# Summing a unit's four neighbour slots by accumulating gathers, with a ring of 16 units, in a three-layer MoE graph network and two attention layers

## The chip, the cores and the metric

One core of a Trainium2 chip. The metric is the device time of one execution in microseconds (us); the median of the timed runs counts. Nothing outside the kernel's one launch is measured.

## The reference, cut to what matters

A graph of N = 6250 nodes and E = 106250 edges sorted by target. Three layers of a mixture of experts each take the mean of the neighbours' hidden rows (256 float32), choose two of eight experts, and add the result to the row. Two attention layers (GAT) follow, the first with four heads.

```python
for l in range(L):                                   # L = 3, h is [N, 256]
    agg = jax.ops.segment_sum(h[src], dst, num_segments=N) / deg
    logits = jnp.concatenate([h, agg], axis=-1) @ router_W[l] + router_b[l]
    vals, idx = jax.lax.top_k(logits, TOPK)
    ...
    h = h + conf * moe
return h @ W_out + b_out
```

```python
e = jax.nn.leaky_relu(alpha_s[src] + alpha_d[dst], NEG_SLOPE)
ex = jnp.exp(e - m[dst])
out = jax.ops.segment_sum(h[src] * alpha[:, :, None], dst, num_segments=n)
```

In the MoE layers only the sum of the neighbours' rows is needed. In the GAT layers each row is weighed with its own softmax weight, so the rows have to arrive one by one.

## The kernel before, in words

**Tiling.** The nodes are sorted by degree and dealt out to 49 groups of 128 nodes (one node to a partition). A group's edges are padded to its own greatest degree and cut into units of four slots (`SLOTS = 4`, line 46). One slot is one indirect DMA: 128 rows, one to a partition, taken from a table in HBM by 128 indices out of `stage`. The trace has 657 real units in the three MoE rounds, 219 to a round (4.47 to a group), filled up to 224 units, which are 896 gathers to a round. There are five such rounds: three of MoE with rows of 256 floats, two of GAT with rows of 136 floats.

**The ring.** `ring` (line 98) holds 32 slots, eight units. GpSimd's queue (POOL) issues the gathers in the loop of lines 466 to 480: unit by unit, slot by slot, each signed off on the unit's own semaphore `gathered[u]`. In the middle of each unit POOL waits twice: at line 473 on `ring_free` (DVE has used up the old contents of the next unit) and at line 475 on `gathered` of the unit before, after which it raises `arrived` for DVE. SyncE (SP) reloads half of `stage` (16 slots) once the units of that half have arrived (lines 358 to 362).

**MoE rounds on DVE.** `aggregate` (lines 686 to 702) starts from the node's own row (line 692), and per unit waits on `arrived`, sums the four slots of the unit with a TENSOR_REDUCE (line 696, which frees the unit), and adds the partial sum to the accumulator in PSUM (line 699). Beside this DVE gates the experts of the group before the last (line 710), adds up the weak experts (line 713), forms the gates of the last group (lines 729 to 749, in which line 738 waits for ACT's exponential), and adds the strong experts to h (line 723). PE transposes the operands of group g (lines 1216 to 1220), runs the first products of group g-1 (line 1243), the router, the weak experts and the second products of group g-2 (line 1284). `fill_up` (line 677) passes over the units of padding at a round's end.

**Between rounds** POOL waits until each group's h is done and scatters it to the next table (line 492: 49 indirect DMAs, line 496 for the GAT tables); the next round's gathers begin when all have landed.

**GAT rounds on DVE.** Per unit a score, a running maximum, the weights (exponential on ACT), the weighing (line 866, which frees the unit) and the sum (line 870). At a group's end comes `turn` (line 872).

```python
                        if b % SLOTS == SLOTS // 2:
                            pool.wait_ge(ring_free, i * UNITS + (b // SLOTS + 2))
                            pool.wait_ge(gathered[(b // SLOTS - 1) % UNITS], i * (16 * SLOTS) + 16 * SLOTS)
                            pool.sem_inc(arrived, 1)
```

Of the kernel before, what the change touches and what calls it, by code (L numbers as in the profile page):

```python
# [26 lines left out]
ALU = mybir.AluOpType  # L27
# [19 lines left out]
RING = 32  # L47
# [20 lines left out]
def gnn_kernel(nc, x, src, dst, W_in, b_in, router_W, router_b, weak_W, weak_b, strong_W1, strong_b1,  # L68
# [3 lines left out]
    with ctx:  # L72
# [25 lines left out]
        ring = sb("ring", [P, RING, H])  # L98
# [4 lines left out]


# [28 lines left out]
        hist = sb("hist", [GROUPS, 3, P])  # L133
# [8 lines left out]
        zeros = sb("zeros", [P, P])  # L142
# [73 lines left out]
        def bank(name):  # L216
# [24 lines left out]
        half_begun, arrived, round_gathered, ring_free, table_done = (sem(n) for n in (  # L241
            "half_begun", "arrived", "round_gathered", "ring_free", "table_done"))
# [30 lines left out]
        def _(sp):  # L273
# [60 lines left out]
            for r in range(LAYERS + 2):  # L334
# [22 lines left out]
                with sp.Fori(1, bodies) as i:  # L357
                    for half in range(2):
                        sp.wait_ge(arrived, total * r + i * UNITS + (r + 1 - UNITS + (half + 1) * UNITS // 2))
                        sp.dma_start(stage[:, half, :], slot_tab[:, bass.ds(i * RING + half * RING // 2, RING // 2)])\  # L360
                            .then_inc(staged[half], 16)
# [4 lines left out]
        def _(pool):  # L366
# [48 lines left out]
            for g in range(GROUPS):  # L415
                pool.indirect_dma_start(out=run_raw[:, g, :], out_offset=None, in_=src.rearrange("(a e) -> a e", a=1),
                                        in_offset=bass.IndirectOffsetOnAxis(ap=perm[:, g, 1:2], axis=1))\
                    .then_inc(gathered[UNITS - 1] if g < SLOTS else s_runs, 16)
# [44 lines left out]
            for r in range(LAYERS + 2):  # L463
                table = hidden_tab[r] if r < LAYERS else gat_tab[r - LAYERS]
                width = H if r < LAYERS else GW
                with pool.Fori(bodies * r, bodies * (r + 1)) as i:  # L466
                    for b in range(RING):
# [3 lines left out]
                        if b % SLOTS == SLOTS // 2:  # L471

                            pool.wait_ge(ring_free, i * UNITS + (b // SLOTS + 2))

                            pool.wait_ge(gathered[(b // SLOTS - 1) % UNITS], i * (16 * SLOTS) + 16 * SLOTS)
                            pool.sem_inc(arrived, 1)
                        pool.indirect_dma_start(out=ring[:, b, 0:width], out_offset=None, in_=table,  # L477
                                                in_offset=bass.IndirectOffsetOnAxis(ap=stage[:, b * 2 // RING, b % (RING // 2):b % (RING // 2) + 1], axis=0))\
                            .then_inc(gathered[b // SLOTS], 16)
                pool.wait_ge(gathered[UNITS - 1], bodies * (16 * SLOTS * (r + 1)) + 16 * SLOTS)  # L480
                pool.sem_inc(arrived, 1)
# [25 lines left out]
        def _(dve):  # L507
# [106 lines left out]
            dve.wait_ge(s_runs, 16 * (GROUPS - SLOTS))  # L614
# [71 lines left out]
            def aggregate(r, g):  # L686
# [6 lines left out]
                with dve.Fori(total * r + c0, total * r + c1) as q:  # L693
                    dve.drain()
                    dve.wait_ge(arrived, q + (r + 2))
# [140 lines left out]
            for k in range(2):  # L836
                r = LAYERS + k

                def rows_of(unit):
                    return ring[:, bass.ds(unit % UNITS * SLOTS, SLOTS), 0:GW]  # L840

                def score_unit(q):

                    dve.wait_ge(arrived, total * LAYERS + q + (r + 2))
# [568 lines left out]
```

## Time and profile before

| what | us |
|---|---|
| median of three timed runs (6931.01 to 6934.34) | 6931.53 |
| span of the profiled execution | 9249.5 |
| set-up until the first gather | 518.5 |
| MoE round, gathers, three times | 1759.3, 1761.2, 1763.0 |
| GAT round, gathers, twice | 1375.8, 1389.1 |
| between the last MoE gather and the first GAT gather | 301.7 |

The profiled execution has no time of its own on record beside its span, so what lies around the span isn't known; the span alone is 2318 us longer than the median of the timed runs. In the tables of the profile a group is all instructions of one line and operation; "idle before" is the time in which that engine did nothing just before them, with what ended it; "issue" means that the profile shows nothing the engine waited for. The DMA_INDIRECT time of POOL is the making of the descriptors, not the transfer.

### The profile page before, as it was taken

Reading aid. Unit: us, or ns where it says so; the run is one execution under the profiler, and the core shown is the slowest. Engines: PE = TensorE matmul, PEld = TensorE weight load, DVE = VectorE, ACT = ScalarE, POOL = GpSimd, SP = SyncE. Lnnn points to the kernel's source line nnn. Section 1 sums busy time; section 2 is a strip of 40 time slices with the busy share of each in tenths; the row PEclk is TensorE's granted clock in tenths of the full one; section 3 lists DMA queues with packets and bytes.
Section 4 is the critical chain, followed back from the end, with each engine's and each line's share of the span. In section 5 each row is a group of like instructions: output and inputs, shape, how many; then the busy total and the mean of one; then the engine's idle time right before and its main releaser. Section 6 shows DMA issues by size and latency. Waiting matters only on the chain. (4 is left out here: it accounts for less than half of the span.)

```text
span 9249.5 us, 91514 instructions
## 1 busy us (share of the span) xinstructions
PE 4191.8 (45%) x21235; PEld 3360.2 (36%) x21235; DVE 4614.2 (50%) x9920; ACT 1371.9 (15%) x4985; POOL 4726.6 (51%) x4956
## 2 busy tenths in 40 slices
PE   6136677676477677763666777772000000000000
PEld 3035566565355555653555565551000000000000
DVE  8225554554255555552455545524555553555554
ACT  2012212221112122221122222221000000000000
POOL 1644444445454444444444444425666666666665
PEclk9567888888688787886788888865555555555555
DMA  1132222223222222232222222211222222222222
GB/s 46 30 89 64 69 69 63 67 66 71 84 71 67 64 68 68 64 64 91 65 68 62 68 65 68 64 22 43 45 46 46 46 45 48 45 46 46 45 45 42
DMA packets 270134, 542.64 MB, mean 59 GB/s; under 512 B 125302, under 2 KB 141881, under 8 KB 269961
## 3 DMA queue, kind: packets, MB, share of 16 engines
q0 software_dynamic: 202832, 511.64, 23.7%
q1 hardware_dynamic: 67260, 30.51, 1.2%
q8 instruction: 19, 0.31, 0.0%
q14 instruction: 23, 0.19, 0.0%
HBM read 510.76 MB, written 31.05 MB: 59 GB/s over the span
## 5 line engine op out<-in xcount | busy, mean ns | idle before, releaser
L477 POOL DMA_INDIRECT ring<-hidden_tab,stage x2688 | 2550.6, 949 | 2811.6 <-DVE part L696 1815.5
L477 POOL DMA_INDIRECT ring<-gat_tab,stage x1792 | 1696.4, 947 | 1073.1 <-issue 543.9
L696 DVE TENSOR_REDUCE part<-ring 128x256 f32 x657 | 1262.1, 1921 | 335.7 <-issue 259.2
L1243 PE MATMUL ps_w1a<-agg_t,wbuf 128*128 128x128 f32 x4704 | 821.0, 335 | 764.7 <-issue 558.3
L1243 PE MATMUL ps_w1b<-agg_t,wbuf 128*128 128x128 f32 x4704 | 838.3, 330 | 618.5 <-issue 500.0
L1284 PE MATMUL ps_moe<-wbuf,strong 128*128 128x256 f32 x4704 | 1057.3, 383 | 0.0
L1243 PEld LDWEIGHTS ps_w1a<-agg_t,wbuf 128*128 128x128 f32 x4704 | 758.4, 247 | 787.6 <-issue 564.9
L1243 PEld LDWEIGHTS ps_w1b<-agg_t,wbuf 128*128 128x128 f32 x4704 | 760.3, 241 | 696.9 <-issue 575.9
L1284 PEld LDWEIGHTS ps_moe<-wbuf,strong 128*128 128x128 f32 x4704 | 883.5, 190 | 163.8 <-issue 48.1
L738 DVE TENSOR_SCALAR gate_n<-ex 128x2 f32<-128x2 f32 x147 | 25.3, 172 | 1783.6 <-ACT ex L1003 1696.0
L870 DVE TENSOR_REDUCE gacc<-strong 128x132 f32<-128x660 f32 x438 | 575.9, 1315 | 23.4 <-issue 15.6
L710 DVE TENSOR_TENSOR strong<-strong,ps_gate 128x512 f32<-128x512 f32 x588 | 363.9, 679 | 204.1 <-PE ps_gate L1272 155.1
L1012 ACT ACTIVATE strong<-ps_w1a,b_t 128x128 f32<-128x128 f32 x1176 | 336.7, 374 | 779.3 <-remote 508.8
L1012 ACT ACTIVATE strong<-ps_w1b,b_t 128x128 f32<-128x128 f32 x1176 | 337.2, 374 | 593.9 <-remote 360.4
L1119 ACT ACTIVATE ps_gate<-shifted 128x20 f32<-128x20 f32 x438 | 83.5, 191 | 2184.0 <-DVEq L858 1137.0
L993 ACT ACTIVATE h_t<-ps_tr 128x256 f32<-128x256 f32 x147 | 56.5, 384 | 2353.3 <-remote 1882.2
L1366 PE MATMUL ps_weak_a<-gat_w,x_t 128*128 128x136 f32 x148 | 60.6, 513 | 760.7 <-ACTq L1100 341.1
L866 DVE TENSOR_TENSOR strong<-ring,ps_gate 128x528 f32<-128x528 f32 x438 | 305.8, 698 | 33.4 <-issue 32.1
L1366 PEld LDWEIGHTS ps_weak_a<-gat_w,x_t 128*128 128x128 f32 x148 | 37.0, 311 | 781.0 <-issue 597.7
L699 DVE TENSOR_TENSOR ps_sum<-ps_sum,part 128x256 f32<-128x256 f32 x657 | 284.0, 432 | 60.6
L713 DVE TENSOR_REDUCE part<-weak 128x256 f32<-128x1024 f32 x147 | 281.0, 1912 | 42.5 <-ACT weak L1024 39.4
L1263 PE MATMUL ps_weak_a<-wbuf,agg_t 128*128 128x512 f32 x588 | 301.3, 638 | 0.0
(273 smaller groups left out, 5444.0 us busy)
## 6 DMA issues: line engine op xcount, KB each, us to landing
ring<-hidden_tab,stage POOLq DMA_INDIRECT x2688
ring<-gat_tab,stage POOLq DMA_INDIRECT x1792
hidden_tab<-h_res SPq DMA_DIRECT2D x49, 128.0 KB, 1.7
wbuf<-in_L_gnn_strong_W SPq DMA_DIRECT2D x6, 1024.0 KB
wbuf<-in_L_gnn_strong_W SPq DMA_DIRECT2D x12, 512.0 KB
stage<-slot_tab SPq DMA_DIRECT2D x280, 8.0 KB
wbuf<-in_L_gnn_weak_W SPq DMA_DIRECT2D x6, 512.0 KB
slot_tab<-wbuf SPq DMA_DIRECT2D x1, 1584.0 KB, 6.0
```

The source lines that it names most:

```text
L477: pool.indirect_dma_start(out=ring[:, b, 0:width], out_offset=None, in_=table, in_offset=bass.IndirectOffsetOnAxis(ap=stage[:, b * 2 // RI ...
L696: nc.vector.tensor_reduce(part[:], ring[:, bass.ds((q % UNITS) * SLOTS, SLOTS), :].rearrange("p s n -> p n s"), AX.X, ALU.add).then_inc(ri ...
L699: nc.vector.tensor_tensor(acc, acc, part[:], ALU.add)
L710: nc.vector.tensor_tensor(strong[odd][:, s, :, :], strong[odd][:, s, :, :], ps_gate[:, s * P:(s + 1) * P].unsqueeze(1).to_broadcast([P, 4, ...
L713: nc.vector.tensor_reduce(part[:], weak[:].rearrange("p e n -> p n e"), AX.X, ALU.add).then_inc(weak_added, 1)
L866: nc.vector.tensor_tensor(terms[:, 0:SLOTS, :, :], rows_of(unit)[:, :, 0:HEADS * HC].rearrange("p s (h c) -> p s h c", c=HC), p[:, 0:SLOTS ...
L870: nc.vector.tensor_reduce(gacc[:].rearrange("p h c -> p (h c)"), terms[:].rearrange("p s h c -> p (h c) s"), AX.X, ALU.add)
L1012: last = nc.scalar.activation(strong[odd][:, s, c, :], ps_w1[s % 2][:, c * P:(c + 1) * P], ACT.Relu, bias=b1_t[:, j:j + 1])
L1243: last = mm(ps_w1[s % 2][:, c * P:(c + 1) * P], w1_w[:, k, s, c * P:(c + 1) * P], agg_t[odd][:, k * P:(k + 1) * P], start=k == 0, stop=k == 1)
L1263: last = mm(ps_weak[j][:], agg_t[odd][:, k * P:(k + 1) * P], wk_w[:, k, j * 512:(j + 1) * 512], start=False, stop=k == 1)
L1284: last = mm(ps_moe[:, 0:H], strong[odd][:, s, c, :], w2_w[:, c, s, :], start=False, stop=s == NS - 1 and c == 3)
L1366: mm(ps_weak[odd][:, 0:P + 2 * HEADS], x1_t[odd][:], gat_w[k][:], start=True, stop=True).then_inc(row_ready, 1)
```

## The change

In the MoE rounds the ring's units become sums. The ring has room for 16 units (`RING = 64`); in a MoE round each unit is one slot of 256 floats. POOL takes half a ring (eight units) at a time and goes through it slot-major: the first slot of all eight units as plain gathers, then the second slot of all eight as gathers that add to what lies in the unit (`compute_op=ALU.add`), then the third and the fourth. Units are taken in pairs. Before each adding gather POOL waits until the gather before it into the same unit has landed. In the fourth pass, before pairs 2, 3 and 4, it waits for the pair that it has just issued and raises `arrived` by 2; the last pair is signed off in the next half, after four more gathers. DVE's `aggregate` loses the TENSOR_REDUCE over four slots, and its addition reads the ring directly and frees the unit. The number of gathers stays 896 a round: a body is 64 gathers and not 32, 14 bodies to a round and not 28. Of a MoE round's 896 gathers 672 add. The GAT rounds keep their order and get 64 slots (16 units) packed at 136 floats. `hist` and `zeros` move into `wbuf` to make room, and SP loads halves of 32 columns of `stage`, 140 loads and not 280.

```diff
-RING = 32
+RING = 64
...
-        ring = sb("ring", [P, RING, H])
+        ring = sb("ring", [P, RING * GW // H, H])
...
+        def early(r):
+            return 2 * min(r + 1, LAYERS) + max(r + 1 - LAYERS, 0)
...
+                def landed(u, i, count):
+                    pool.wait_ge(gathered[u], i * (16 * SLOTS) + (16 * count + (16 * SLOTS if u >= UNITS - 2 else 0)))
...
+                def sum_units(i, half):
+                    pool.wait_ge(staged[half], i * 16 + 16)
+                    pool.sem_inc(half_begun, 1)
+                    for j in range(SLOTS):
+                        for u in range(0, UNITS // 2, 2):
+                            n = half * UNITS // 2 + u
+                            if j == 0:
+                                if u == 4:
+                                    for k in range(2):
+                                        landed(n - 6 + k if half else UNITS - 2 + k, i, SLOTS if half else 0)
+                                    pool.sem_inc(arrived, 2)
+                                pool.wait_ge(ring_free, i * UNITS + (n + 2))
+                                pool.sem_inc(unit_open, 1)
+                                for k in range(2):
+                                    into(ring[:, n + k, :], half, (u + k) * SLOTS).then_inc(gathered[n + k], 16)
+                                continue
+                            if j == SLOTS - 1 and u:
+                                for k in range(2):
+                                    landed(n - 2 + k, i, SLOTS)
+                                pool.sem_inc(arrived, 2)
+                            for k in range(2):
+                                landed(n + k, i, j)
+                            pool.sem_inc(unit_open, 1)
+                            for k in range(2):
+                                pool.indirect_dma_start(
+                                    out=ring[:, n + k, :], out_offset=None, in_=table,
+                                    in_offset=bass.IndirectOffsetOnAxis(ap=stage[:, half, (u + k) * SLOTS + j:(u + k) * SLOTS + j + 1], axis=0),
+                                    compute_op=ALU.add).then_inc(gathered[n + k], 16)
...
-                    dve.wait_ge(arrived, q + (r + 2))
-                    nc.vector.tensor_reduce(part[:], ring[:, bass.ds((q % UNITS) * SLOTS, SLOTS), :].rearrange("p s n -> p n s"),
-                                            AX.X, ALU.add).then_inc(ring_free, 1)
-                    dve.drain()
-                    nc.vector.tensor_tensor(acc, acc, part[:], ALU.add)
+                    dve.wait_ge(arrived, q + (early(r) + 1))
+                    nc.vector.tensor_tensor(acc, acc, ring[:, bass.ds(q % UNITS, 1), :].rearrange("p a n -> p (a n)"), ALU.add)\
+                        .then_inc(ring_free, 1)
```

## Rows read from the trace of the kernel before

**Rows 1.** The page of the profiled execution: span, busy times of the engines.
```profile
span 9249.5 us, 91514 instructions
...
PE 4191.8 (45%) x21235; PEld 3360.2 (36%) x21235; DVE 4614.2 (50%) x9920; ACT 1371.9 (15%) x4985; POOL 4726.6 (51%) x4956
```

**Rows 2.** Waits of POOL: who waited for whom, us in total, times, longest.
```profile
POOL ring L477 <- DVE part L696: 1815.5, 145, 30.9
...
POOL ring L477 <- DVE strong L866: 449.5, 88, 11.9
```

**Rows 3.** Groups by line, POOL: busy us, mean ns | idle before.
```profile
L477 POOL DMA_INDIRECT ring<-hidden_tab,stage x2688 | 2550.6, 949 | 2811.6 <-DVE part L696 1815.5 <-issue 812.7 <-DMA ring<-hidden_tab,stage 104.8
L477 POOL DMA_INDIRECT ring<-gat_tab,stage x1792 | 1696.4, 947 | 1073.1 <-issue 543.9 <-DVE strong L866 449.5 <-DMA ring<-gat_tab,stage 79.7
L492 POOL DMA_INDIRECT hidden_tab<-h_res,perm x98 | 94.4, 963 | 102.0 <-DVE h_res L723 65.2 <-issue 28.1 <-DMA ring<-hidden_tab,stage 8.7
...
L422 POOL DMA_INDIRECT h_res<-hidden_tab,perm x49 | 57.2, 1168 | 14.9 <-issue 14.9
```

**Rows 4.** Windows of MoE round 2 and both GAT rounds, line 477 alone: POOL busy, clock, DMA share.
```profile
4269.20:6032.20 1763.00, 850.52 (x896) 0.80 0.27 67
6333.90:7709.70 1375.80, 848.48 (x896) 0.50 0.25 46
7777.90:9167.00 1389.10, 847.95 (x896) 0.50 0.25 45
```

**Rows 5.** Timeline of POOL, MoE round 0: gathers at three body ends.
```profile
2079.49 0.95 POOL L477 DMA_INDIRECT ring<-hidden_tab,stage  x1 [1.72 <-issue]
...
2115.42 0.95 POOL L477 DMA_INDIRECT ring<-hidden_tab,stage  x1 [1.31 <-issue]
...
2153.91 0.94 POOL L477 DMA_INDIRECT ring<-hidden_tab,stage  x1 [1.09 <-issue]
```

**Rows 6.** Timeline of PE in a stretch where its matmuls start slowly.
```profile
3023.62 0.37 PE L1243 MATMUL ps_w1b<-agg_t,wbuf 128*128 128x128 f32 x1 [1.83 <-issue]
...
3025.76 0.37 PE L1243 MATMUL ps_w1b<-agg_t,wbuf 128*128 128x128 f32 x1 [1.76 <-issue]
```

**Rows 7.** Timeline, one undisturbed MoE group of five units: PE, DVE, POOL.
```profile
794.50 0.27 PE L1219 MATMUL ps_tr<-ident,agg 128*128 128x128 f32 x1
...
804.03 1.92 DVE L696 TENSOR_REDUCE part<-ring 128x256 f32 x1 [0.32 <-issue]
...
806.78 0.95 POOL L477 DMA_INDIRECT ring<-hidden_tab,stage  x1 [26.20 <-DVE part L696]
806.79 1.91 DVE L696 TENSOR_REDUCE part<-ring 128x256 f32 x1 [0.31 <-issue]
...
809.01 7.17 PE L1284 MATMUL ps_moe<-wbuf,strong 128*128 128x256 f32 x32
...
818.21 0.33 PE L1219 MATMUL ps_tr<-ident,agg 128*128 128x128 f32 x1 [1.81 <-issue]
```

**Rows 8.** Groups by line, DVE: the sum over slots and its addition.
```profile
L696 DVE TENSOR_REDUCE part<-ring 128x256 f32 x657 | 1262.1, 1921 | 335.7 <-issue 259.2 <-POOLq L476 76.4
...
L699 DVE TENSOR_TENSOR ps_sum<-ps_sum,part 128x256 f32<-128x256 f32 x657 | 284.0, 432 | 60.6
```

**Rows 9.** Timeline of DVE, first GAT round: two units, then the end of a group.
```profile
7209.45 0.17 DVE L845 TENSOR_TENSOR score<-ring,ad_cur 128x16 f32<-128x16 f32 x1 [0.65 <-issue]
...
7213.16 0.17 DVE L845 TENSOR_TENSOR score<-ring,ad_cur 128x16 f32<-128x16 f32 x1 [0.41 <-issue]
...
7221.18 1.33 DVE L870 TENSOR_REDUCE gacc<-strong 128x132 f32<-128x660 f32 x1
...
7227.51 0.29 DVE L865 TENSOR_TENSOR strong<-gacc,ps_gate 128x132 f32<-128x132 f32 x1 [0.36 <-ACT ps_gate L1119]
```

**Rows 10.** Timeline of POOL at the end of MoE round 0.
```profile
2281.95 1.00 POOL L492 DMA_INDIRECT hidden_tab<-h_res,perm  x1 [4.14 <-DMA ring<-hidden_tab,stage]
```

**Rows 11.** DMA issues: median us from issue to landing.
```profile
meta_tab<-meta,rank_i POOLq DMA_INDIRECT x49, 2.1
```

More of the change, by code:

```diff
@@ L102, in gnn_kernel @@
         ad = [sb(f"ad{i}", [P, GROUPS, HEADS]) for i in range(2)]
+        gat_ring = ring[:].rearrange("p a n -> p (a n)").rearrange("p (s n) -> p s n", n=GW)
         wbuf = sb("wbuf", [P, 10240])
@@ L132, in gnn_kernel @@
         hi_b = ring[:, 6:8, :].rearrange("p a b -> p (a b)").bitcast(BF16)[:, 0:ET]
-        hist = sb("hist", [GROUPS, 3, P])
+        z_at = d_at + GROUPS * P // 2
+        hist = wbuf[0:GROUPS, z_at:z_at + 3 * P].rearrange("p (a n) -> p a n", n=P)
         row_pre = sb("row_pre", [GROUPS, 1])
@@ L141, in gnn_kernel @@
         bkt_base = sb("bkt_base", [P, GROUPS])
-        zeros = sb("zeros", [P, P])
+        zeros = wbuf[:, z_at + 3 * P:z_at + 4 * P]
         rank = sb("rank", [P, GROUPS])
@@ L417, in _ @@
                                         in_offset=bass.IndirectOffsetOnAxis(ap=perm[:, g, 1:2], axis=1))\
-                    .then_inc(gathered[UNITS - 1] if g < SLOTS else s_runs, 16)
+                    .then_inc(gathered[UNITS - 1 - g // SLOTS] if g < 2 * SLOTS else s_runs, 16)
             pool.wait_ge(s_h0st, 16 * GROUPS)
@@ L464, in _, with into @@
                 table = hidden_tab[r] if r < LAYERS else gat_tab[r - LAYERS]
-                width = H if r < LAYERS else GW
-                with pool.Fori(bodies * r, bodies * (r + 1)) as i:
+                def landed(u, i, count):
+                    pool.wait_ge(gathered[u], i * (16 * SLOTS) + (16 * count + (16 * SLOTS if u >= UNITS - 2 else 0)))
+                def into(tile, half, k):
+                    return pool.indirect_dma_start(
+                        out=tile, out_offset=None, in_=table,
+                        in_offset=bass.IndirectOffsetOnAxis(ap=stage[:, half, k:k + 1], axis=0))
@@ L473, in _ @@
                             pool.wait_ge(ring_free, i * UNITS + (b // SLOTS + 2))
-                            pool.wait_ge(gathered[(b // SLOTS - 1) % UNITS], i * (16 * SLOTS) + 16 * SLOTS)
+                            landed((b // SLOTS - 1) % UNITS, i, SLOTS if b >= SLOTS else 0)
                             pool.sem_inc(arrived, 1)
[L477 to L481, printed above, removed]
+                        into(gat_ring[:, b, :], b * 2 // RING, b % (RING // 2)).then_inc(gathered[b // SLOTS], 16)
+                with pool.Fori(bodies * r, bodies * (r + 1)) as i:
+                    if r < LAYERS:
+                        sum_units(i, 0)
+                        sum_units(i, 1)
+                    else:
+                        raw_slots(i)
+                for u in range(UNITS - (2 if r < LAYERS else 1), UNITS):
+                    pool.wait_ge(gathered[u], bodies * (16 * SLOTS * (r + 1)) + 16 * SLOTS)
+                    pool.sem_inc(arrived, 1)
                 pool.sem_inc(round_gathered, 1)
@@ L839, in rows_of @@
                 def rows_of(unit):
-                    return ring[:, bass.ds(unit % UNITS * SLOTS, SLOTS), 0:GW]
+                    return gat_ring[:, bass.ds(unit % UNITS * SLOTS, SLOTS), :]
                 def score_unit(q):
-                    dve.wait_ge(arrived, total * LAYERS + q + (r + 2))
+                    dve.wait_ge(arrived, total * LAYERS + q + (early(r) + 1))
                     nc.vector.tensor_tensor(score[:, 0:SLOTS, :], rows_of(q)[:, :, GW - HEADS:GW],
```

12 lines of the change are left out of this document (7 added, 5 removed).

## The prediction

> **What bounds the kernel now.** I read the page first, then POOL's waits, its groups by line, the windows of the five rounds, and last the timelines. The page shows no engine above 51% [rows 1], which says little here: all work hangs on 4480 gathers that only POOL issues. A gather costs POOL 0.95 us, plus 0.30 us before the next (543.9 us of "issue" before 1792 GAT gathers), so 1.25 us [rows 3], so 896 of them are 1120 us. A MoE round takes 1763 us and the GAT rounds 1376 and 1389 us [rows 4]. What is over is mostly POOL waiting for DVE to free ring units: 1815.5 us before the MoE gathers, 449.5 us before the GAT gathers [rows 2].
>
> Taken at its word, the profile says that DVE's chain bounds the MoE rounds, and that taking the TENSOR_REDUCE off DVE must pay. But the timed median is 6931.5 us against a span of 9249.5 us [rows 1], so 2318 us of this execution do not exist in the timed runs, and I have to decide which. In the profile PE has long stretches in which one matmul of 0.27 or 0.37 us starts every 2.1 us and waits for nothing shown [rows 6]; ACT and DVE wait behind it. Where these are absent, a group of five units goes from transpose to transpose in 818.21 - 794.50 = 23.7 us [rows 7]. POOL's own time without its waits for DVE is 9249.5 - 1815.5 - 449.5 = 6984.5 us [rows 1, 2], 0.8% above the timed median. I take this as the main reading: **in the timed runs POOL hardly ever waits for DVE, and POOL's issue is the bound.** The undisturbed chain fits: it is 23.7 - 5 x 2.76 = 9.9 us plus 2.76 us a unit (from a reduce of 1.92 and an addition of 0.43 with their gaps [rows 7, 8]), 22.2 us for the mean group of 4.47 units, while POOL needs 224 x 4 x 1.25 / 49 = 22.9 us a group. GAT: 3.7 us a unit and some 5 us at a group's end [rows 9] give 21.6 us against the same 22.9. The engines are close to balance, with POOL last.
>
> **The change, part by part,** against the timed 6931.5 us (the profiled execution comes at the end of this part).
>
> DVE: 657 reduces of 1.92 us and about 0.31 us of gap go [rows 8], 657 x 2.23 = 1465 us of DVE time. Where POOL is the bound this is worth nothing: POOL's issue hides it. If that cover were gone it would be worth up to what the next engine allows: PE's undisturbed step ends with line 1284 at 816.18, 21.7 us after the transpose at 794.50 [rows 7].
>
> Gathers: 896 to a round as before. 672 of each MoE round's now add, 2016 in all. The trace has no adding DMA. Lower bound of the extra issue cost 0: the gathers and the scatters of rows 3 take 947 to 963 ns, whatever the direction. Upper bound from the dearest indirect DMA, line 422, at 1168 ns [rows 3]: 0.22 us x 2016 = 443 us. I take 0, since nearly all rows sit there, and keep 443 for the range.
>
> The new waits: in the fourth pass POOL waits, before pairs 2, 3 and 4, for the pair that it has just issued. Behind this wait stand POOL's own next gathers, with nothing else to issue, so its whole length lies on the bound. There are 3 x 28 halves x 3 rounds = 252. The length: after its last gather of a round POOL stands idle 4.14 us, instead of 0.30, until the landing lets it go on [rows 10], but this holds a loop exit too. From below: an indirect DMA lands 2.1 us after issue [rows 11], 1.1 us after the 0.96 us record ends; from DVE's release (reduce ended 804.03 + 1.92 = 805.95) to POOL's next gather at 806.78 passes 0.83 us [rows 7]; together 1.9 us idle, 1.6 more than 0.30. From above: the old wait on the unit before comes after two further gathers, 0.30 + 0.95 + 0.30 + 0.95 + 0.30 = 2.8 us after the unit's last gather, and delays nothing (the idle times that a landing ends are 104.8 us before all MoE gathers [rows 3]), so 2.5 more for a plain gather; the round's end gives 3.8. An adding gather can only land later. I take 2.2 us, between the nearer two: 252 x 2.2 = 554 us. Bounds 1.6 and 3.8: 403 and 958 us.
>
> The other waits between passes: eight gathers, 10 us, lie between two into the same unit, so they are covered. The last pair of a half is signed off after four gathers, 5 us: covered, unless an adding gather lands over 5 us late. Their semaphore and register instructions run in POOL's sequencer beside the 0.95 us of the gather before; the old ones add nothing to the 0.30 us [rows 3].
>
> Bodies: a body end costs 1.09 to 1.72 us in place of 0.30 [rows 5]; I take 1.1 over the usual. 14 fewer in each of five rounds: 70 x 1.1 = 77 us less. SP's stage loads, 140 instead of 280, are asked for a half ring ahead (40 us) and cost nothing either way.
>
> Supply to DVE: eight units come at the end of each half instead of one every 5 us, so a MoE round starts some 30 us later on DVE. POOL's 40 us of the next half hide this; at a round's end the last half brings only three real units, and the 49 scatters (61 us) cover the tail. GAT: the deeper ring can remove waits, but by the main reading few are left: 0, at most 50 us. `hist` and `zeros` in `wbuf`: set-up only, 0.
>
> **Sum:** 6931.5 + 554 - 77 = 7408, say **7410 us, 6.9% slower**. For the profiled execution the signs differ: DVE's chain gives up 489 us a MoE round and would pass 1270 us, where POOL then needs 1120 + 28 x 3 x 2.2 + 14 x 1.1 = 1320; with both in each other's way 1400. Its span would be about 9249.5 - 3 x 360 = 8170 us: a shorter profile and a longer timed run.
>
> **Transfer cost of adding.** The 16 DMA engines are busy 0.27 of 1763 us for 896 gathers, 0.53 us each, against an issue every 1.25 us [rows 4]. Twice the read work, or even double the whole, would be 1.06 us and still fit. The Trainium skill, in "Collectives: The Full Stack", section "The bandwidth ceiling: the fold count and why AG ≠ RS ≠ AR", speaks against this change: an adding transfer reads two sources for each write, and the reading side sets the rate. No row here shows an adding transfer. By that rule the exposed landings would come up to 0.53 us later each, 134 us more than my sum.
>
> **The rivals.**
>
> Adding gathers cost more than plain ones (0.22). Either POOL takes longer to make their descriptors or the DMA engines do not keep up; all gathers queue behind. For: an addition needs a read of the ring besides. Against: the flat 947 to 963 ns and the slack of the DMA engines [rows 3, 4]. At 0.22 us each, 7408 + 443 = 7850 us; at twice that, 8300 us.
>
> DVE's chain is the bound in the timed runs too (0.17), the other side. Then POOL's gather must be quicker without the profiler than 1.25 us, and the agreement 6984 to 6931 would be chance. Decides: POOL at or under about 1.0 us a gather. POOL then needs 224 x 4 + 28 x 3 x 2.2 = 1081 us a round, and PE is the bound at 22 us a group, 1080 us. The round before is about 1145 us: counted over line 696, 27 groups of up to four units at PE's 22 us, 15 of five at 23.7, and seven of six to nine at 9.9 + 2.76 a unit. After, PE's 1078 and a later start of some 25 make 1100. Gain: 3 x 45 = 135, and about 35 in the GAT rounds: 6760 us. For: groups of up to four units need 22 us of PE and DVE against at most 20 of POOL, and the profile's largest wait is this one.
>
> It evens out (0.05): the gain on large groups and bodies pays for short waits, 6930 us. That the gathers would not add at all, so that nothing waits, is in here: POOL waits on their semaphores whatever they do.
>
> **How the numbers follow.** My own case has 0.56 and its own range is 7180 (waits of 1.6 us, deeper GAT ring) to 7850 (waits of 3.8 us, or descriptors of 1168 ns). The range reaches down to the DVE case and up into the dear gathers: 6760 to 8050. Left out are half of the DVE case and those gathers that cost over 0.3 us more, together under 0.2. Faster by over 0.2%: 0.18; within 0.2% (about what the timing can tell from no change): 0.04; slower: 0.78.
>
> **What would show it.** Right: adding gathers at about 950 ns; 252 idle times of about 2.5 us before them, ended by the landing; POOL waiting for DVE far less than 1815 us; MoE rounds of about 1400 us and a shorter span, with a longer timed run. Wrong: adding gathers well above 950 ns (second case); a timed run that falls with the span (third case); idle times before the fourth pass near 0.3 us, which would leave the change free.

## The result, and the profile after

The changed kernel takes 8688.24 us (median of 3 runs, 8686.14 to 8694.94) against 6931.53 us: a ratio of 1.2533, 95% interval 1.2511 to 1.2556. It is slower, as forecast, but by 1757 us where 480 were forecast, and outside the range. Its profiled execution took 8686.14 us, so here the profile and the timed runs agree.

The page of after, against [rows 1]; the second line is busy time:

```profile
span 8684.6 us, 89965 instructions
...
PE 3792.3 (44%) x21235; PEld 3073.7 (35%) x21235; DVE 3353.3 (39%) x9263; ACT 1382.2 (16%) x4985; POOL 5920.2 (68%) x4956
```

DVE gave up 1261 us of work. POOL, with the same 4956 instructions, got 1194 us more. The groups by line of POOL (busy us, mean ns | idle before), against [rows 3]; line 504 is the adding gather:

```profile
L504 POOL DMA_INDIRECT ring<-hidden_tab,stage x2016 | 3105.3, 1540 | 1358.6 <-DMA ring<-hidden_tab,stage 961.2 <-issue 393.7 <-DVE ps_sum L744 3.7
L476 POOL DMA_INDIRECT ring<-gat_tab,stage x1792 | 1694.3, 945 | 654.9 <-issue 542.5 <-DMA ring<-gat_tab,stage 110.3 <-DVE strong L912 1.8
L476 POOL DMA_INDIRECT ring<-hidden_tab,stage x672 | 642.0, 955 | 236.8 <-issue 183.2 <-DMA ring<-hidden_tab,stage 46.6 <-DVE ps_sum L744 7.0
```

An adding gather holds POOL for 1540 ns, a plain one for 945 to 955. And 961.2 us of idle time end with a landing, where before had 104.8; 821 of them are the 252 exposed waits at a mean of 3.26 us each, the rest is the usual gap of 0.30 us put down to a landing. Before its gathers POOL waits for DVE for 12.5 us in all. The timeline of POOL at the end of one half's fourth pass shows the exposed waits:

```profile
2065.50 1.54 POOL L504 DMA_INDIRECT ring<-hidden_tab,stage  x1 [3.09 <-DMA ring<-hidden_tab,stage]
2067.34 1.54 POOL L504 DMA_INDIRECT ring<-hidden_tab,stage  x1 [0.30 <-issue]
2072.01 1.54 POOL L504 DMA_INDIRECT ring<-hidden_tab,stage  x1 [3.12 <-DMA ring<-hidden_tab,stage]
...
2079.04 1.54 POOL L504 DMA_INDIRECT ring<-hidden_tab,stage  x1 [3.65 <-DMA ring<-hidden_tab,stage]
```

Between two gathers of a pair stand 0.30 us, before the next pair 3.1 to 3.7 us: pairs 2, 3 and 4, three waits in each of 84 halves. The DMA engines carry the same bytes in nearly twice the packets. The line of the software queue (packets, MB, share of the 16 engines' span) in the profile of before, then of after:

```profile
q0 software_dynamic: 202832, 511.64, 23.7%
```

```profile
q0 software_dynamic: 396368, 511.64, 34.9%
```

The difference is 193536 packets, 96 for each of the 2016 adding gathers. The windows of a MoE round and of the first GAT round (length, POOL busy, clock, DMA share, GB/s), against [rows 4]:

```profile
4178.90:5947.20 1768.30, 1248.83 (x896) 0.80 0.42 67
6192.80:7361.50 1168.70, 845.54 (x896) 0.50 0.29 54
```

By these rows alone the MoE rounds cost what they cost in the profile of before (1763 us), and the two GAT rounds (1168.7 and 1175.8 us) got some 210 us shorter each. That is the trap of this case: the two profiles were taken where the chip behaved differently.

**The kernel before has two levels.** A number can't be understood here without this: on some chips every run of before took 6925 to 6970 us, on others 9215 to 9440 us. The timed runs of before and all those of after behind the ratio above are of the first kind, and so is after's profile; the profile of before (9249.5 us) is of the second. I call them chips of the first and of the second kind. (One execution of experiment 13, on a chip of the first kind, took 8830.98 us at a granted clock of 0.537 and stands outside its ratio.) The kernel before, profiled on a chip of the first kind (experiment 12, below), gives the comparison that counts: the page's span, then POOL's gathers of the MoE rounds, then the window of one MoE round.

```profile
span 6937.1 us, 91367 instructions
```

```profile
L477 POOL DMA_INDIRECT ring<-hidden_tab,stage x2688 | 2544.4, 947 | 1046.1 <-issue 811.4 <-DMA ring<-hidden_tab,stage 163.8 <-DVE part L696 41.4
```

```profile
3017.90:4205.60 1187.70, 848.09 (x896) 0.95 0.39 99
```

POOL waits for DVE for 41.4 us instead of 1815.5, a MoE round is 1188 us instead of 1763, and the GAT rounds (1169.2 and 1172.4 us) are those of after. So the whole difference lies in the MoE rounds: 1182.0 + 1188.9 + 1187.7 = 3558.6 us before, 1771.9 + 1769.5 + 1768.3 = 5309.7 us after, 1751 us more, of a difference in span of 8684.6 - 6937.1 = 1747.5. Split by POOL's busy and idle time it is:

| | before | after | difference |
|---|---|---|---|
| POOL busy in the three MoE rounds | 2544.4 | 3747.3 | +1203 (2016 x 0.593 = 1195 of it) |
| idle beyond 0.30 us a gather | 209 | 757 | +548: the exposed waits 252 x 2.95 = 744, less the 209 of before |

### The profile page after: what moved, and what is told of

It is laid out like the page before. It is cut to its first block and busy times, and to the rows that moved or that the text cites. A ratio compares the mean times of both kernels' runs of the same rounds, so it can differ in the third digit from the quotient of the medians.

```text
span 8684.6 us, 89965 instructions
## 1 busy us (share of the span) xinstructions
PE 3792.3 (44%) x21235; PEld 3073.7 (35%) x21235; DVE 3353.3 (39%) x9263; ACT 1382.2 (16%) x4985; POOL 5920.2 (68%) x4956
## 5 line engine op out<-in xcount | busy, mean ns | idle before, releaser
L504 POOL DMA_INDIRECT ring<-hidden_tab,stage x2016 | 3105.3, 1540 | 1358.6 <-DMA ring<-hidden_tab,stage 961.2
L744 DVE TENSOR_TENSOR ps_sum<-ps_sum,ring 128x256 f32<-128x256 f32 x657 | 284.3, 433 | 2963.8 <-POOLq L499 2782.7
L1265 PE MATMUL ps_tr<-ident,agg 128*128 128x128 f32 x147 | 56.8, 387 | 2019.6 <-DVE agg L748 2019.6
L476 POOL DMA_INDIRECT ring<-hidden_tab,stage x672 | 642.0, 955 | 236.8 <-issue 183.2
L1265 PEld LDWEIGHTS ps_tr<-ident,agg 128*128 128x128 f32 x147 | 24.0, 163 | 2040.0 <-DVE agg L748 2040.0
L1289 PE MATMUL ps_w1a<-agg_t,wbuf 128*128 128x128 f32 x4704 | 706.8, 315 | 0.0
L1289 PEld LDWEIGHTS ps_w1a<-agg_t,wbuf 128*128 128x128 f32 x4704 | 683.9, 231 | 0.3
L1289 PE MATMUL ps_w1b<-agg_t,wbuf 128*128 128x128 f32 x4704 | 606.0, 285 | 0.0
L1289 PEld LDWEIGHTS ps_w1b<-agg_t,wbuf 128*128 128x128 f32 x4704 | 588.1, 203 | 0.0
```

The lines of the kernel that those rows point to most:

```text
L476: return pool.indirect_dma_start(out=tile, out_offset=None, in_=table, in_offset=bass.IndirectOffsetOnAxis(ap=stage[:, half, k:k + 1], axi ...
L504: pool.indirect_dma_start(out=ring[:, n + k, :], out_offset=None, in_=table, in_offset=bass.IndirectOffsetOnAxis(ap=stage[:, half, (u + k) ...
L744: nc.vector.tensor_tensor(acc, acc, ring[:, bass.ds(q % UNITS, 1), :].rearrange("p a n -> p (a n)"), ALU.add)\
L1289: last = mm(ps_w1[s % 2][:, c * P:(c + 1) * P], w1_w[:, k, s, c * P:(c + 1) * P], agg_t[odd][:, k * P:(k + 1) * P], start=k == 0, stop=k == 1)
```

## The experiments

**1, 12. The kernel before again, for its profile.** No edit. On a chip of the second kind:

> The kernel before, once more, for its profile. Theory 1 (in undisturbed executions POOL's issue of gathers is the bound, and the waits for DVE in the first profile belong to that one execution): span about 6930 us, 4480 gathers still at 0.95 + 0.30 us, POOL's waits for lines 696 and 866 together under 250 us instead of 2265. Theory 2 (DVE's chain is the bound in the timed runs, POOL is quicker than 1.25 us a gather there): gathers at 1.05 us or less from start to start and waits for DVE above 600 us in all.

It took 9404.57 us: theory 1's number missed, with 1946.9 us of waits for DVE before the MoE gathers, and so did theory 2, as the gathers kept their 0.95 + 0.30 us. That began the question of the two levels. Later, on a chip of the first kind:

> The kernel before once more, for its profile. Theory: where it takes about 6930 us, its MoE rounds are bound by POOL, about 1120 to 1150 us each (896 gathers at 1.25 us), the GAT rounds about 1150 to 1180, POOL's waits for DVE below 150 us in all and no group of PE with more than 50 us of idle time put down to issue. Where it takes 9250 to 9400 us it shows again what the first profile shows: rounds of 1760 to 1800 us and about 1000 us of such idle time.

6938.65 us, with the rows shown above. MoE rounds came at 1182 to 1189 us (1120 to 1150 expected: the small waits, below). The groups of PE by line show what differs; first the second kind, then the first:

```profile
L1243 PE MATMUL ps_w1a<-agg_t,wbuf 128*128 128x128 f32 x4704 | 836.9, 339 | 881.0 <-issue 535.6 <-ACT strong L1012 345.0
L1243 PE MATMUL ps_w1b<-agg_t,wbuf 128*128 128x128 f32 x4704 | 836.2, 327 | 696.5 <-issue 627.8 <-ACT strong L1012 66.0
```

```profile
L1243 PE MATMUL ps_w1a<-agg_t,wbuf 128*128 128x128 f32 x4704 | 627.8, 291 | 0.0
L1243 PE MATMUL ps_w1b<-agg_t,wbuf 128*128 128x128 f32 x4704 | 590.9, 280 | 0.0
```

The same matmuls, in the same order, lose 1163 us to starts that wait for nothing shown [rows 6], and on the other chip none. That these late starts become POOL's waits for DVE, by way of ACT and DVE, is inferred from this comparison. The mean granted clock of a MoE round differs too, 0.80 against 0.95, but by itself it doesn't bring the late starts: after on a chip of the first kind also has 0.80, and its page gives these matmuls 0.0 us of idle time.

**2, 13. No reduce, and nothing in its place.** DVE adds a unit's first slot only; the other three slots are gathered but not summed.

```
-  nc.vector.tensor_reduce(part[:], ring[... SLOTS ...], AX.X, ALU.add).then_inc(ring_free, 1)
-  dve.drain()
-  nc.vector.tensor_tensor(acc, acc, part[:], ALU.add)
+  nc.vector.tensor_tensor(acc, acc, ring[... 1 ...], ALU.add).then_inc(ring_free, 1)
```

> The kernel before without the sum over the four slots of a unit in the MoE rounds: DVE adds slot 0 alone, so three of four neighbour rows are left out; all gathers stay. Takes 657 reduces, some 1465 us, off DVE. Theory 1 (POOL's issue is the bound): 6931 less at most 120 us, so 6810 to 6930. Theory 2 (DVE's chain is the bound in the MoE rounds): down to what PE allows, 6750 or less.

On the second kind: 9229.04 us, ratio 0.9803 (0.9786 to 0.9819), with 1772.1 us of POOL's waits for DVE still there. 1465 us of DVE's time were worth 183 us.

> The kernel before without DVE's sum over the four slots (it adds the first slot of a unit alone; 657 sums of 1.92 us and drains gone). Theory where before takes about 6930 us (POOL's issue of gathers bounds the MoE rounds): a round cannot fall below 896 x 1.25 = 1120 us, and 1186 were measured, so at most 3 x 66 = 200 us go, and of them only what waits for DVE's slots, 41.4 us by the profile, with the small waits of POOL that come with DVE's hold on the ring: 6790 to 6900 us, ratio 0.98 to 0.995. Rival (DVE has a part in the bound after all): more than 200 us faster, below 6730. Where before takes 9230 to 9400 us: ratio 0.98 again, as measured.

On the first kind: 6952.7 us against 6956.18, ratio 0.9994 (0.9984 to 1.0004). The reduce was worth nothing at all (6790 to 6900 us had been expected): only 2.4 us of waits for DVE are left before POOL's MoE gathers, and DVE waits 940.9 us for POOL instead of 195.8. The rounds keep 1180 to 1183 us, so their small waits are not waits for DVE either.

**3. The change with plain gathers.** `compute_op=ALU.add` goes, so the rows overwrite each other; order, waits and ring are those of after.

> The changed kernel with the 2016 adding gathers as plain ones, same order and same waits; each unit then holds its last slot alone, the other three rows are left out. Theory 1 (an adding gather costs POOL 1540 ns in place of 950, 2016 x 0.59 = 1190 us, and lands later): 8688 - 1190 - 252 x 0.6 = about 7350 us, idle time before the fourth pass's pairs about 2.5 us each. Rival (slot-major order, the more numerous waits or the longer loop body make the gathers dear, not the adding): above 8200 us.

9408.18 us, ratio 0.9991 (0.9976 to 1.0006), second kind.

```profile
L504 POOL DMA_INDIRECT ring<-hidden_tab,stage x2016 | 1906.6, 946 | 1274.2 <-issue 696.9 <-DMA ring<-hidden_tab,stage 573.9 <-DVE ps_sum L743 3.4
```

The gathers of line 504 went back to 946 ns: it is the addition that costs, not the order. The 252 exposed waits hardly fell. In the timeline they have a mean of 2.92 us (2.61 to 4.08), against 3.25 us in experiment 5, the change itself on this kind of chip; the profile puts 99 of them down to "issue", which is why the sum ended by landings looks smaller. POOL also waited 1279.6 us for DVE again, so the total says nothing on the 7350 us expected.

**4, 11. The change, with a unit handed over one pair later**: in the fourth pass POOL waits for the last pair but one (u - 4 in place of u - 2), so that two more gathers, one pair, stand between a gather and the wait for it. The last two pairs of a half are waited for in the next half, behind four gathers each. (The expectation of experiment 11 calls this two pairs later.)

```
-  if j == SLOTS - 1 and u:
+  if j == SLOTS - 1 and u >= 4:
       for k in range(2):
-          landed(n - 2 + k, i, SLOTS)
+          landed(n - 4 + k, i, SLOTS)
       pool.sem_inc(arrived, 2)
```

(the ends of the halves and of a round, and the counts of `early`, follow from that.)

> The changed kernel with each pair signed off two gathers later in the fourth pass (pair u-4 instead of u-2, the last two pairs of a half in the next half), so that POOL waits for no gather it has just issued. Adding gathers stay. Theory 1 (252 exposed waits of 3.27 us, 2.97 us over the usual 0.30, lie whole on the bound): 8688 - 748 = about 7940 us. Rival (the DMA engines cannot keep up with adding gathers, so that the wait only moves to the next place): 8500 us or more.

Second kind: 8611.01 us, ratio 0.9144 (0.9129 to 0.916). The time is in the rival's range, but only because this chip is of the second kind; the MoE rounds decide. They took 1522.4, 1522.2 and 1521.9 us, with no idle time above 0.4 us: 1770 - 1522 = 248 a round, 744 in all for the 252 waits, 2.95 us each.

> The kernel after, with a unit handed to DVE two pairs later, again, beside another set of runs of before. Theory (it is bound by POOL in the MoE rounds whatever the level the chip runs at, 1522 us a round): 8550 to 8650 us where before takes 9250 to 9400 us (ratio 0.91 to 0.93); where before takes 6930 us, 8688 - 3 x 248 = 7944 us, 7900 to 7990, ratio 1.14 to 1.15. Rival (the level of a chip adds to every kernel alike, about 1.35 times): 8600 us in the first case, but about 6400 in the second.

First kind: 7956.54 us, ratio 1.1482 (1.1463 to 1.1501), where 7944 had been expected from 8688 - 744. This settles the price of the waits. It also shows that POOL bounds the MoE rounds of after on both kinds. POOL's group of adding gathers there:

```profile
L504 POOL DMA_INDIRECT ring<-hidden_tab,stage x2016 | 3107.8, 1542 | 614.3 <-issue 369.9 <-DMA ring<-hidden_tab,stage 241.3 <-DVE ps_sum L746 3.0
```

The idle time is 614.3 / 2016 = 0.30 us before each: nothing but the usual gap, although 241.3 of it are put down to a landing.

**5. The changed kernel again.**

> The changed kernel unchanged, beside the kernel before on the same chip, since the kernel before took 9412 us in the last four runs and 6931 us in the first comparison. Theory D (the kernel before has two levels, one in which PE, ACT and DVE start instructions late while plain gathers run, one without; adding gathers hardly provoke it): where before is near 9412, this is about 9100 to 9360 us (MoE rounds 1770 us, POOL-bound as in its first profile, GAT rounds 1390 in place of 1172), thus faster than before; where before is near 6931, this is 8688. Rival (the changed kernel has the same two levels with the same 2480 us between them): about 11100 us beside 9412.

Second kind: 9274.57 us against 9254.91, ratio 1.0018 (1.0003 to 1.0032), in the range of theory D, though not faster than before. The MoE rounds (1771.9, 1768.9, 1769.2) are those of the first kind; the GAT rounds (1354.8, 1383.6) and the scatters (94 us against 62) are longer. So the change is a quarter slower on one kind of chip and costs next to nothing (0.2%) on the other, where before's MoE rounds are as long (1759 to 1803 us) because of its waits for DVE.

**6, 16. The GAT ring of 64 slots alone**, with the MoE rounds of before.

```
-  if r < LAYERS:
-      sum_units(i, 0); sum_units(i, 1)
-  else:
-      raw_slots(i)
+  raw_slots(i, r < LAYERS)
```

> Only the GAT part of the change: MoE rounds as before (plain gathers, sum of four slots on DVE, eight units in flight), GAT rounds with 64 slots, bodies of 64 gathers. Theory 1 (POOL's issue bounds the undisturbed GAT rounds, the ring is deep enough): where before is near 6931, 6931 less 77 us of body ends, 6850 to 6930. Where before is near 9412, DVE bounds the GAT rounds at 28 us a group and a deeper ring only shifts the wait: within 0.5% of before. Rival (the shallow ring costs waits even there): over 100 us less.

> The MoE rounds of before, the GAT ring of 64 slots of after. Where before takes about 6930 us: theory, the GAT rounds are bound by POOL's issue of 896 gathers at 1.25 us (1120 us, about 1170 with the ends of the loop's bodies) with either ring, since POOL waits 3 us for DVE there: time within 0.3% of before, GAT rounds of 1165 to 1180 us. Rival (half as many loop bodies save an end each, some 1.5 us of idle time, 28 a round): 40 to 80 us faster, ratio 0.988 to 0.994. Where before takes 9250 us: ratio 0.999 again, as measured.

Both met chips of the second kind: ratios 0.999 (0.9972 to 1.0007) and 1.0003 (0.9988 to 1.0019). On the first kind it wasn't run alone, but there the GAT rounds of after (1168.7, 1175.8) and of before (1169.2, 1172.4) are alike: the deeper ring is worth nothing.

**7. Plain gathers and the later hand-over together.**

> The changed kernel with plain gathers in place of adding ones and with the late sign-off, so without the two costs of the change; three of four neighbour rows are left out. Theory 1: where before is near 6931, the body-end gain is all that is left, 6850 to 6950 us. Where before is near 9412: MoE rounds of 1750 us as in the run with plain gathers and the early sign-off, 9300 to 9420 us, which would show that there the waits of POOL are not what bounds them.

Second kind: 9612.08 us, ratio 1.0389 (1.0363 to 1.0416), MoE rounds of 1827 to 1831 us (1750 expected). With the cheaper gathers it is 1001 us slower than experiment 4 (on another chip of that kind, where before took 157 us less). One of PE's groups shows where:

```profile
L1290 PE MATMUL ps_w1b<-agg_t,wbuf 128*128 128x128 f32 x4704 | 826.0, 306 | 1131.5 <-issue 1126.9 <-ACT strong L1059 2.8
```

That gave the theory that closely issued gathers make the other engines start late.

**8. Before, with gathers slowed by drains.**

```
+  if r < LAYERS:
+      for _ in range(2):
+          pool.drain()
+          nc.gpsimd.memset(zeros[:], 0.0)
```

> The kernel before, with two drains and two writes of the 128x128 tile zeros (196 ns each for such a write in the profile of before) by POOL behind every gather of the MoE rounds: plain gathers, but one every 1.7 to 1.85 us instead of every 1.25 us, 896 of them in a round, so POOL needs about 1530 to 1660 us a round; it now waits some 600 us a round for DVE. Theory (the late starts of PE, ACT and DVE come from plain gathers that follow each other at 1.25 us, and the adding gathers of after avoid them by being slower): MoE rounds of about 1600 to 1680 us instead of 1760 to 1800, PE's idle time put down to issue in these rounds at half or less, and a time 3 to 6% below before (about 8850 to 9050 where before takes 9250 to 9400). Rival A (the late starts have nothing to do with the gathers' spacing): the waits for DVE take up the added time, rounds within 1% of before or up to 5% longer, time the same or up to 3% more. Rival B (on a chip where before takes 6930 us): the added 0.45 to 0.6 us x 2688 shows in full, 8150 to 8550 us.

14800.33 us, ratio 1.5972 (1.5946 to 1.5999), second kind: no case foresaw this. POOL stands idle 1.92 us where a drain follows a gather, and a gather is issued every 4.1 us in the mean. It isn't a test at the spacing wanted (1.7 to 1.85 us), but at 4.1 us the two groups of PE's hidden layer (line 1247 there) have 0.0 us of idle time.

**9. The disputed cost by itself.** Behind the last round of after, with the other engines idle, four series of 24 gathers and four of 8 where each is waited for.

```
+  row_by_row(hidden_tab[0], wide, False)
+  row_by_row(hidden_tab[0], wide, True)
+  row_by_row(gat_tab[0], slim, False)
+  row_by_row(gat_tab[0], slim, True)
...
+  row_by_row(hidden_tab[0], wide[0:1] * 8, True, True)
```

> The kernel after, and behind its last round, with the other engines idle: 24 gathers of each of four kinds to tiles of their own (plain and adding, rows of 1024 bytes and of 544 bytes), then 8 of each kind to one tile, each waited for before the next is issued. Theory (an adding gather costs POOL more for each of its 128 rows, as the other engines' work has nothing to do with it): adding about 1540 ns and plain about 950 ns, for both widths, to within 40 ns; from issue to landing some 1.2 us more for the adding one with the wide rows (3.8 us against 2.6 in the rounds). Rival (the added time is the DMA engines' write with addition pushing back on POOL, so bytes count): the adding gather of 544 bytes takes about 1260 ns (950 + 590 x 544/1024), or in the idle chip both fall to 950. Second rival (contention for memory with the other engines makes 1540 of 950): all four kinds at 950 here.

The groups by line in the windows of an adding series with rows of 1024 bytes, a plain and an adding one with 544 bytes:

```profile
L559 POOL DMA_INDIRECT ring<-hidden_tab,stage x20 | 30.8, 1540 | 6.1 <-issue 6.1
...
L559 POOL DMA_INDIRECT ring<-gat_tab,stage x24 | 22.8, 948 | 9.4 <-issue 7.0 <-DMA ring<-hidden_tab,stage 2.4
...
L559 POOL DMA_INDIRECT ring<-gat_tab,stage x19 | 29.3, 1542 | 7.8 <-issue 7.8
```

1540 and 1542 ns, whatever the width, with the other engines idle: the price is paid in POOL, and neither bytes nor contention make it. All these gathers have 128 rows, so no run tells whether it goes by the row or by the gather. The packets of the software queue in the windows of these series do differ: 144 for an adding gather of either width, 48 for a plain one with 1024-byte rows, 32 with 544-byte rows. Plain gathers of 48 and of 32 packets hold POOL equally long (0.95 us). Timeline of the waited-for series, wide adding and wide plain:

```profile
9462.58 1.54 POOL L559 DMA_INDIRECT ring<-hidden_tab,stage  x1 [2.56 <-DMA ring<-hidden_tab,stage]
...
9491.49 0.95 POOL L559 DMA_INDIRECT ring<-hidden_tab,stage  x1 [2.06 <-DMA ring<-hidden_tab,stage]
```

Behind POOL's own part an adding gather takes 2.5 us to land and to be answered, a plain one 2.07: 0.4 us more with 1024 bytes, and by the same view 2.06 against 1.87 with 544. The expectation had put this difference at 1.2 us. In the rounds the adding gather's wait is 2.95 + 0.30 = 3.25 us.

**10, 14, 15. Before, with gathers slowed by four short writes**: one gather every 1.43 us at the closest instead of 1.25 (1.46 in the mean of a round on the first kind), where the first expectation had hoped for 1.75 to 2.1.

```
+  if r < LAYERS:
+      pool.wait_ge(paced, i * (RING * 4) + (b * 4 + 4))
+      pool.sem_inc(pace_seen, 1)
+      for k in range(4):
+          nc.gpsimd.memset(zeros[:, k * 32:k * 32 + 32], 0.0).then_inc(paced, 1)
```

> The kernel before, with four writes of 32 columns each of the tile zeros by POOL behind every gather of the MoE rounds, this time with no drain (the drains took 1.92 us each and made a gather of every 4.1 us). A write of few columns took about 0.1 us in the profile of before, so with its issue some 0.5 to 0.8 us are added: a plain gather every 1.75 to 2.1 us, a round of 896 needs 1570 to 1880 us of POOL. Theory (PE, ACT and DVE start late because plain gathers follow each other at 1.25 us; in the drained variant, at 4.1 us, PE's idle time put down to issue fell from some 1160 us to nothing in the two groups of the hidden layer): that idle time at a third or less of the 1058 us that L1243 shows in the profile of before, and MoE rounds that last no longer than POOL needs, about 1600 to 1700 us where the writes come to 0.5 us, against 1760 to 1800. Rival (only a spacing near 4 us, or adding gathers, spare the other engines): the idle time stays above 700 us, the rounds at 1760 to 1900 us. If before takes about 6930 us on this chip, its issue time is small from the start, and this kernel takes 8300 to 9200 us.

> The kernel before with four short writes by POOL behind every gather of the MoE rounds (a gather every 1.46 us instead of 1.25 us). Theory where before takes 9230 to 9400 us (dense plain gathers make the other engines start late): PE's idle time put down to issue in the group of L1251 well under the 1058 us of before, and MoE rounds shorter than 1760 to 1800 us, 1500 to 1700, in spite of POOL's added work. Rival (spacing up to 1.5 us changes nothing): rounds of 1760 to 1850 us, time within 1% of before or up to 3% more. Where before takes 6930 us: 7320 to 7360 us again.

First kind, twice (10 and 14): ratios 1.0559 (1.0541 to 1.0577) and 1.0573 (1.0556 to 1.0591), some 390 us more, as POOL's slower issue shows. Second kind, one run (15): 8637.81 us where before takes 9250.97: 858 us of writes more on POOL, and 613 us less of time. MoE rounds of 1572.6, 1565.4 and 1542.9 us, and the group of PE:

```profile
L1251 PE MATMUL ps_w1a<-agg_t,wbuf 128*128 128x128 f32 x4704 | 738.3, 321 | 532.8 <-issue 297.9 <-ACT strong L1020 234.8
L1251 PE MATMUL ps_w1b<-agg_t,wbuf 128*128 128x128 f32 x4704 | 691.7, 306 | 238.8 <-ACT strong L1020 141.0 <-issue 97.1
```

Of these two groups' late starts 395 us are left, where experiment 16, with the MoE rounds of before on the same chip, has 1129.5: about a third.

**17, 18. Before with a unit handed over one unit later** (and the GAT ring of 64 slots), meant to beat both kernels.

```
-  landed((b // SLOTS - 1) % UNITS, i, SLOTS if b >= SLOTS else 0)
+  landed((b // SLOTS - 2) % UNITS, i, SLOTS if b >= 2 * SLOTS else 0)
```

> Plain gathers and DVE's reduce in the MoE rounds as before, the GAT ring of 64 slots, and one thing new: POOL waits for the landing of the unit two back instead of one back, and hands it to DVE then. Theory where before takes about 6930 us (the idle times of 0.5 to 2.6 us before a unit's third gather are waits for a late landing, about 70 us in a MoE round and 50 in a GAT round): they vanish, MoE rounds of 1120 to 1130 us instead of 1182 to 1189, GAT rounds of 1120 to 1130 instead of 1169 to 1172, and 6931 - 3 x 62 - 2 x 48 = 6650 us, 6600 to 6750, ratio 0.952 to 0.974: faster than both kernels. Rival (they are waits for DVE to free a unit, or DVE is too close to the bound): the idle times stay with DVE as their releaser, ratio 0.99 to 1.0. Where before takes 9230 to 9400 us: other engines bound the rounds, ratio 0.99 to 1.02, and the idle times ended by a landing (about 105 us before the MoE gathers) go.

Both runs met the second kind: ratios 1.0108 (1.0079 to 1.0137) and 1.0104 (1.0064 to 1.0144), with POOL waiting 2070.1 and 2119.1 us for DVE. One thing they do show: idle times above 0.4 us before a gather that DVE did not end, 41 to 43 in a MoE round of experiment 6, are gone in both, but for one of 0.5 us in two of the three rounds. These were waits for the landing of the unit before. What removing them is worth on the first kind, where it was aimed at, is open.

## Why the prediction was wrong, and where it was right

**The bound: right.** "In the timed runs POOL hardly ever waits for DVE" came out as 41.4 us, and the reduce as worth nothing (0.9994). The comparison of span less waits with the timed median (6984 to 6931) had found the right state of the chip without a trace of it. That it came as near as 0.8% was in part luck: the same subtraction in the profile of experiment 12 gives 6937.1 - 44.4 = 6892.7 us, and the passages between rounds, 149 us longer in the profile of before, make up for it. The expected round was 1120 plus ends; it is 1188.

**The issue cost of an adding gather: the step that failed.** I took 0 and called 0.22 us the upper bound, from line 422. It is 0.593 us, 1195 us in all. The bound was none: the rows of [rows 3] all copy, so they say nothing on a gather that also reads its destination. The rival that named the cost had the right engine (POOL is held longer by each adding gather) and a third of the price; even its doubled form, 0.44 us, fell short. The page that I cited, "Collectives: The Full Stack" of the Trainium skill, in "The bandwidth ceiling: the fold count and why AG ≠ RS ≠ AR", says that a reducing transfer gives two read descriptors where a copy gives one. I applied it to the transfer only. Applied to POOL, two reads and a write in place of one of each would be an estimate, by that section, of 1.5 x 0.947 = 1.42 us; measured are 1.54. That the extra time is the making of a third descriptor is not shown by a run. That it doesn't go by bytes is (experiment 9), and that adding gathers leave 144 packets where plain ones leave 48 or 32 is a second possible cause, which no run separates from the first.

**The exposed waits: right in place and number, small in size.** 252 were forecast, and 252 are there; I gave 2.2 us each, they are 2.95, so 744 us instead of 554, inside the bounds of 1.6 and 3.8. Two things make up the 0.75 us. With plain gathers in the same places (experiment 3) the wait is already 2.62 us beyond the usual gap, so the lean to the nearer of the two estimates cost 0.42. The addition costs the other 0.33, or 0.4 in the waited-for series of experiment 9. The sentence that by the rule of the Trainium skill the landings would come up to 0.53 us later fits that. So does the transfer itself: by the windows (0.42 of 1768.3 us, less 224 plain gathers at 0.39 x 1187.7 / 896 = 0.52 us) an adding gather keeps the DMA engines busy for an estimated 0.93 us, well under the 1.84 us between two. As forecast, the DMA engines keep up.

**The bodies: misread.** The 77 us do not exist. In the trace of before on a chip of the first kind a body's first gather has 0.305 us of idle time before it, as every other. The rows that I took for body ends [rows 5] are, counted from 0, gathers 26, 14 and 2 of a body, each the third of a unit: there POOL waits for the landing of the unit before, which I had costed at nothing. The timeline of experiment 3 (second kind) shows why that wait isn't always covered: a plain gather that is waited for at once lets POOL go on after 2.61 to 4.08 us, and the two gathers in between take 2.80 with their gaps. The small waits come to 65 to 72 us a MoE round, 209 in all, of which 29 end with DVE. Most fall at the same gathers in every round (22, 50, 66, 82, 118, ..., counted from 0), so they hang on what those units gather; what makes those land late I do not know. With the wait put off by a unit they vanish (experiments 17 and 18). In after's MoE rounds they are gone. The lower end of my own range was mis-added besides: 6931.5 + 403 - 77 - 50 is 7208, not 7180. With the right sizes the sum is 6931.5 + 1203 + 744 - 209 = 8670 us, 19 below the measured.

**The foretold profile: wrong by its assumption.** I expected a shorter span (8170 us), with MoE rounds of 1400 us, from an execution as disturbed as the profile of before. After's profile came from an undisturbed chip; on a disturbed one (experiment 5) its span is 9278.9 us, as POOL takes 1769 to 1772 us for a MoE round there too, with its waits for landings.

**The rivals.** The DVE-bound case is refuted for the first kind (0.9994 without the reduce). On the second kind DVE and PE do bound the rounds, but by late starts that a shorter DVE chain does not remove (0.9803).

## What to carry to other kernels

Put a profile's own time beside the timed runs before arguing from it; where the two differ, as here by a third, say which waits the timed runs can't hold, and don't set a later profile against it before both are of the same level. On a kernel bound by gathers issued one by one, count what each costs its issuer: taking the sum off an engine that was hidden (1465 us) put 1195 us on the one that sets the time. Where no row shows an operation, the dearest relative is no upper bound; and a wait that is to be covered needs the landing's length in gathers between it and its issue. Here two adding gathers, 3.98 us with their gaps, cover it, two plain ones, 2.80 us, do so for most units, and none leaves 2.95 us open.

Of the versions run on the first kind of chip, none beats before. On the second, the change with the later hand-over (0.9144 of before) beats both before and the change (1.0018).

## What was not expected of the hardware

- An adding indirect gather of 128 rows holds GpSimd 1540 ns, a plain one 947 ns, for rows of 1024 and of 544 bytes alike. The adding one leaves 144 packets in the trace for either width, the plain one 48 and 32, with the same bytes.
- The same kernel takes 6930 to 6960 us on some chips and 9250 to 9410 us on others (medians). On the latter PE, ACT and DVE start instructions late with nothing shown that they wait for, mostly by 1 to 4 us. In PE's two groups of the hidden layer this comes to 951 to 1508 us in the nine profiles with plain gathers at 1.25 us, to 395 at 1.43 us, to 65 to 230 with adding gathers at 1.84 us (experiments 5, 9 and 4), and to none at 4.1 us. That the spacing of the gathers is the cause is a theory that these runs fit, and it covers PE only: before DVE's addition the idle time put down to issue is greater in experiment 4 (344.6 us) than on a chip of the first kind (164.4 in experiment 11). Why a chip does this was not found.
- Where a drain follows an indirect gather GpSimd stands idle for 1.92 us; two drains and two writes per gather brought the interval between gathers to 4.1 us.
